# Four destinations side by side in one stationary operand for the last chunk of a count-matrix product

## The chip, the cores and the metric

The kernel runs on one core of a Trainium2 chip, as one program with one launch. The metric is device time in microseconds (us) for the whole program; lower is better. Outputs must agree with a JAX reference in float32.

## The reference, cut to what matters

Four graph-neural-network layers run one after the other on 3125 nodes with 128 features and 50000 edges, which are sorted by destination. Each is wrapped as `x = x + layer(relu(layernorm(x)))`. Layers 1 and 2 weight their edges by a softmax. Layer 0 (called gcn) and the two convolutions of layer 3 (sage1, sage2) need only a plain sum over the edges of each destination:

```python
h = features * rsqrt(max(deg_out, 1))[:, None]
h = h @ W
agg = segment_sum(h[edge_src], edge_dst)          # gcn
gcn_out = agg * rsqrt(max(deg_in, 1))[:, None] + b
...
agg = segment_sum(x[src], dst)                    # sage, twice
agg = agg / maximum(cnt, 1)[:, None]
h = agg @ Wl.T + x @ Wr.T + b
```

## The kernel before, in words

**Steps and chunks.** Destinations are taken in groups of `DG` = 4 (782 groups). The edges lie in 392 blocks of 128. A step is one pair of an edge block and a destination group, walked in order, so there are `STEPS` = 1172 steps. A chunk is 128 steps; there are `NC` = 10 chunks, and the last holds only 20 steps (24 with the padding of its last batch).

**The count matrix.** For every step and each of its four destinations `dl`, a column of the count matrix says how often each source node occurs. A chunk is stored as `adj[p, t*DG+dl, s]`: source node `t*128+p` (25 tiles `t`), destination `dl`, step `s`. TensorE builds it from one-hot vectors in 147 batches of 8 steps (L1389), ScalarE copies each batch into `adj` (L1015), which has two chunk buffers, and SyncE stores each finished chunk to `adj_hbm` (L700, 3200 KB each) for the layers that come later.

**The product.** A unit is one (chunk, `dl`) pair: 25 matmuls with `adj[:, ch, t*4+dl, :]` as the stationary operand (128 by 128) and node features, split in three bf16 parts, as the moving operand. In gcn (`spmm`, L1378) it streams 385 columns, the last of which gives counts. The ten chunks make 40 units, of which units 0 to 31 are placed between the build batches and units 32 to 39 run after the last batch. Before unit 39 the TensorE queue has the count products `degrees` (L1399) of chunks 0 to 8; that of chunk 9 follows after the last unit. VectorE takes each unit's result out of PSUM in `v_row` (a one-column copy, L1958, and a sum of the three parts, L1959). There are four PSUM banks for units, so unit n waits for `v_row(n-3)` to be counted in `v_done`.

**Selection.** `sel` (L1965, L1968) writes 0/1 matrices that say to which destination group each step belongs; `pick` (TensorE, L1449, 112 matmuls in float32) multiplies by them, which puts the sums in node order in `agg_t`. ScalarE copies its first four results out, VectorE the last four (L1975).

**The sage layers.** `load_adj` (SyncE, L819) streams the count matrix back from `adj_hbm` in 5 pieces a chunk, each 5 source tiles with their four destinations (640 KB), through a ring of `RING` = 9 buffers: 50 pieces a layer. A piece is loaded when the piece nine before it has been used (`spmm_done`). `stream` (L1468) runs 20 matmuls a piece, 1000 a layer, with four PSUM banks for even chunks and four for odd ones; VectorE reduces the four banks of a chunk after its last piece (L2386), and `pick` follows when all ten chunks are reduced.

**Between them** lie three edge passes (attn, gat1, gat2) of 98 groups of 512 edges, in which GpSimd gathers four blocks of rows a group (L984). Each engine has one queue, in program order; they meet in semaphores. The order of steps inside the layers is written out in tables of turns.

Of the kernel before, what the change touches and what calls it, by code (L numbers as in the profile page):

```python
# [6 lines left out]
F32 = mybir.dt.float32  # L7
BF16 = mybir.dt.bfloat16
# [5 lines left out]
P = 128  # L14
# [3 lines left out]
TURN = 4  # L18
# [26 lines left out]
PER = P // BATCH  # L45
NC = -(-STEPS // P)
SPAN = [(max(0, c * P - (CH - 2)), min(NGRP, (c + 1) * P)) for c in range(NC)]
SPAN_AT = [sum(b - a for a, b in SPAN[:c]) for c in range(NC + 1)]
HI = 5
NPR = NG // 2  # L50
# [6 lines left out]
HTURNS = -(-CH // WIDE)  # L57
DEG_LATE = NC - 1
RING = 9
assert NG % 2 == 0 and CH % QA == 0 and CQ <= P  # L60

# [94 lines left out]
def gnn_stack_kernel(nc, out, x, src, dst, edge_attr_64, **w):  # L156
    ctx = ExitStack()
    with ctx:
# [114 lines left out]
        def place(at, parts, *dims):  # L273
# [76 lines left out]
        late = carve(arena, {"v_rows": (P, (NC, DG, D), F32), "xs": (P, (NT, 3, D), BF16),  # L350
                             "sel": (P, (SPAN_AT[NC],), F32)}, late_v)
# [3 lines left out]
        sels = carve(arena, {"sel": (P, (SPAN_AT[NC],), F32), "sel_b": (P, (SPAN_AT[NC],), BF16)}, work_at)  # L355
        sel_early, sel_b = sels["sel"], sels["sel_b"]
# [65 lines left out]
        v_done = sem("v_done")  # L422
        sel_done = sem("sel_done")
        picked = sem("picked")
# [163 lines left out]
        def _(sp):  # L588
# [225 lines left out]
            def load_adj(i):  # L814

                def piece(n):
                    if i or n >= RING:
                        sp.wait_ge(spmm_done, NC * DG + i * NC * PIECES + n - RING + 1)
                    sp.dma_start(ring[:, (i * NC * PIECES + n) % RING, :],  # L819
                                 adj_hbm[n // PIECES, :, n % PIECES * HI * DG * P:(n % PIECES + 1) * HI * DG * P])\  # L820
                      .then_inc(adj_in[(i * NC * PIECES + n) % RING], 16)

                for n in range(NC * PIECES):
                    piece(n)

# [14 lines left out]
        def _(pool):  # L840
# [170 lines left out]
        def _(act):  # L1011
# [291 lines left out]
        def _(pe):  # L1303
# [126 lines left out]
            def pick(i, p):  # L1430

                pe.wait_ge(sel_done, i + 1)
                pe.wait_ge(v_done, [NC * DG, NC * DG + NC, NC * DG + 2 * NC][i])
                for half in range(2):
                    for dl in range(DG):
# [10 lines left out]
                        for ch in use:  # L1446
                            a0, a1 = max(SPAN[ch][0], g0), min(SPAN[ch][1], g1)
                            off = SPAN_AT[ch] - SPAN[ch][0]
                            i_ = mm(bank(half * 4 + dl)[:, a0 - g0:a1 - g0], v_of[p][:, ch, dl, :],  # L1449
                                    sel_of[p][:, off + a0:off + a1], start=ch == use[0], stop=ch == use[-1],  # L1450
                                    skip_group_check=True)
# [3 lines left out]
            def stream(i):  # L1455
                for n in range(NC * PIECES):
                    u = i * NC * PIECES + n
                    ch = n // PIECES
                    pe.wait_ge(adj_in[u % RING], 16 * (u // RING + 1))
                    if ch == 0:  # L1460
                        stage = "gat2" if i == 0 else "sage1"
                        pe.wait_ge(dve_o.sem, dve_o.at(stage, "r2", ((n + 1) * HI - 1) // TURN))
                    if n % PIECES == 0 and ch >= 2:
                        pe.wait_ge(v_done, NC * DG + i * NC + ch - 1)
                    for t in range(HI):
                        for dl in range(DG):
                            h = n % PIECES * HI + t
                            m = mm(bank(ch % 2 * 4 + dl)[:, 0:3 * D], ring[:, u % RING, (t * DG + dl) * P:(t * DG + dl + 1) * P],  # L1468
                                   xs1[:, h, :, :].rearrange("p s c -> p (s c)"), start=h == 0, stop=h == NT - 1)
                    m.then_inc(spmm_done, 1)  # L1470
# [259 lines left out]
        def _(dve):  # L1730
# [225 lines left out]
            def v_row(n):  # L1956
                dve.wait_ge(spmm_done, n + 1)
                v.tensor_copy(vdeg[:, n // DG, n % DG:n % DG + 1], bank(4 + n % 4)[:, 3 * D:3 * D + 1])  # L1958
                v.reduce_sum(v_early[:, n // DG, n % DG, :],  # L1959
                             bank(4 + n % 4)[:, 0:3 * D].rearrange("p (s c) -> p c s", s=3), axis=AX_X).then_inc(v_done, 1)  # L1960

            def sel(p):
                for ch in range(NC):
                    g0, g1 = SPAN[ch]
                    i = ts(sel_of[p][:, SPAN_AT[ch]:SPAN_AT[ch + 1]], grp_row[:, 0:g1 - g0], step_f[:, 1, ch:ch + 1], None,  # L1965
                           ALU.is_equal)
                    if p == "gcn":
# [31 lines left out]
            sel("gcn")  # L1999
            for k in range(done, NC * DG):  # L2000
                v_row(k)
# [378 lines left out]
            for i, p in enumerate(("sage1", "sage2")):  # L2380
                if i == 1:
                    dve.sem_inc(sel_done, 1)
                for ch in range(NC):
                    dve.wait_ge(spmm_done, NC * DG + (i * NC + ch + 1) * PIECES)
                    for dl in range(DG):
                        k = v.reduce_sum(v_late[:, ch, dl, :],  # L2386
# [44 lines left out]
```

## Time and profile before

| what | value |
|---|---|
| median of 3 runs | 3070.86 us |
| the three runs | 3072.97, 3061.61, 3070.86 us |
| the profiled execution, its own time | 3065.77 us |
| span of its trace | 3064.1 us |
| mean granted TensorE clock in it | 0.784 of full speed |
| TensorE busy | 2446.2 us (80%) |
| GpSimd busy | 1359.0 us (44%) |
| VectorE busy | 1385.8 us (45%) |

The span is from the first to the last instruction. Times inside it are counted from its start. PE is TensorE's matmul queue, PEld its weight loads, DVE is VectorE, ACT ScalarE, POOL GpSimd, SPq SyncE's queue of transfers. A line such as L1468 names the source line. An idle time stands in brackets, with what ended it. In the chain of waits each row is a piece of the path that ended last: its start, its length, and what ran.

### The profile page before, as it was taken

The numbers are of one execution on the slowest core, as the hardware profiler recorded it, in microseconds if no ns is written. First come the engines' busy times: TensorE is split into PE (matmuls) and PEld (weight loads), VectorE is DVE, ScalarE is ACT, GpSimd is POOL, SyncE is SP. The second block draws the span as 40 slices with busy tenths as digits, with TensorE's granted clock in tenths as the row PEclk, the third lists the DMA queues.
The fourth block names the chain that finished last, engine by engine and source line by source line (L and its number), as shares of the span: only waits on it lengthen the run. The fifth ranks groups of instructions, "written<-read, shape, count | busy, mean of one in ns | idle before, by whom it ended". The sixth has DMA issues, their size and how long they took to land.

```text
span 3064.1 us, 36766 instructions
## 1 busy us (share of the span) xinstructions
PE 2446.2 (80%) x12590; PEld 1810.7 (59%) x12590; DVE 1385.8 (45%) x3000; ACT 929.0 (30%) x1990; POOL 1359.0 (44%) x1416
## 2 busy tenths in 40 slices
PE   5699999848888897667788886666777775699998
PEld 5466666627777775455555554346777775366566
DVE  7655655356676766434445444232222223411313
ACT  4322222133333332543444443322222222201101
POOL 3000000077777773447777772437777773300000
PEclk7577778878898887767999998785555555799999
DMA  9877754039999995106777775205555553664460
GB/s 188 230 258 274 240 179 188 1 98 273 266 261 263 261 256 147 30 20 187 242 242 237 243 246 166 76 19 126 133 133 131 135 134 74 200 201 128 146 203 25
DMA packets 519442, 525.15 MB, mean 171 GB/s; under 512 B 154208, under 2 KB 463843, under 8 KB 517947
## 3 DMA queue, kind: packets, MB, share of 16 engines
q1 hardware_dynamic: 311425, 274.71, 30.1%
q0 software_dynamic: 50528, 115.22, 15.2%
q10 hardware_dynamic: 157306, 132.88, 13.8%
q8 instruction: 103, 1.69, 0.2%
q14 instruction: 80, 0.66, 0.1%
HBM read 306.05 MB, written 229.79 MB: 175 GB/s over the span
## 4 chain that ended last, share of the span: by engine, by line
PE 35%; POOL 32%; issue 13%; DVE 10%; DMA 5%; ACT 4%; another core or an unknown queue 1%; SPq 0%; POOLq 0%; PEldq 0%; DVEq 0%; ACTq 0%
POOL arena L984 30%; PE ps L1468 10%; PE ps L1378 7%; PE ps L1389 6%; DMA arena<-t_gat,src_i 3%; PE ps L1449 2%; DMA arena<-t_attn,src_i 2%; PE ps L1541 1%; PE ps L1665 1%; DVE arena L2160 1%; DVE arena L1840 1%; ACT arena L1015 1%; PE ps L1574 1%; PE ps L1704 1%; ACT arena L1258 1%
## 5 line engine op out<-in xcount | busy, mean ns | idle before, releaser
L1015 ACT ACTIVATE arena<-ps 128x544 f32<-128x544 f32 (+8 forms) x589 | 481.2, 826 | 1636.2 <-PE ps L1541 643.1
L984 POOL DMA_INDIRECT arena<-t_gat,src_i x784 | 740.6, 945 | 239.0 <-issue 233.5
L1541 PE MATMUL ps<-arena 128*128 128x136 f32 (+2 forms) x2352 | 649.7, 436 | 111.2 <-ACT arena L1015 57.5
L1541 PEld LDWEIGHTS ps<-arena 128*128 128x128 f32 x2352 | 447.2, 253 | 242.3 <-DVE arena L2160 89.1
L984 POOL DMA_INDIRECT arena<-t_attn,src_i x392 | 383.4, 978 | 119.5 <-issue 116.4
L1468 PE MATMUL ps<-arena 128*128 128x384 bf16 x2000 | 333.0, 331 | 33.9 <-DVE rec L2302 32.6
L1517 PEld LDWEIGHTS ps<-arena 128*128 128x128 f32 x1568 | 286.6, 267 | 32.2 <-ACT arena L1015 4.7
L1468 PEld LDWEIGHTS ps<-arena 128*128 128x128 bf16 x2000 | 197.9, 99 | 168.8 <-issue 43.0
L2108 DVE TENSOR_TENSOR z_b<-arena,ps 128x12 f32<-128x12 f32 (+1 forms) x196 | 31.5, 161 | 561.7 <-DMA arena<-t_gat,src_i 505.5
L1517 PE MATMUL ps<-arena 128*128 128x3 f32 (+1 forms) x1568 | 266.1, 292 | 4.2 <-ACT arena L1015 4.2
L947 POOL TENSOR_TENSOR arena<-arena,r_L_gnn_gamma 128x512 f32<-128x512 f32 (+1 forms) x7 | 8.0, 1150 | 556.9 <-ACT arena L1197 556.8
L1389 PE MATMUL ps<-arena 128*128 128x100 bf16 x1176 | 225.0, 364 | 27.7 <-DVE arena L1944 27.6
L1378 PE MATMUL ps<-arena 128*128 128x385 bf16 x1000 | 233.8, 407 | 0.0
L2160 DVE TENSOR_TENSOR arena<-arena,ps 128x1536 f32<-128x1536 f32 (+1 forms) x196 | 229.9, 1215 | 3.2 <-ACT arena L1134 2.5
L1389 PEld LDWEIGHTS ps<-arena 128*128 128x128 bf16 x1176 | 169.1, 146 | 78.3 <-DVE arena L1944 31.9
L1525 PE MATMUL ps<-ident,logit 128*64 128x128 f32 (+2 forms) x147 | 46.9, 319 | 172.9 <-DVE logit L2121 108.1
L1378 PEld LDWEIGHTS ps<-arena 128*128 128x128 bf16 x1000 | 119.6, 120 | 108.2 <-issue 69.2
L1015 ACT ACTIVATE arena<-same_b 128x512 f32<-128x512 bf16 x294 | 168.0, 620 | 25.4 <-DMA same_b<-same_hbm 25.3
L2098 DVE TENSOR_TENSOR arena<-arena,ps 128x1024 f32<-128x1024 f32 x98 | 119.1, 1215 | 122.3 <-DMA arena<-t_attn,src_i 93.3
L2386 DVE TENSOR_REDUCE arena<-ps 128x128 f32<-128x384 f32 x80 | 39.0, 549 | 274.1 <-PE ps L1468 274.1
L1525 PEld LDWEIGHTS ps<-ident,logit 128*64 128x64 f32 (+2 forms) x147 | 18.4, 125 | 183.1 <-DVE logit L2121 113.3
L1501 PE MATMUL ps<-w_e,arena 64*128 64x128 f32 x784 | 123.3, 302 | 0.7 <-DVE arena L2098 0.7
(315 smaller groups left out, 2930.3 us busy)
## 6 DMA issues: line engine op xcount, KB each, us to landing
ends_gat<-arena ACTq DMA_DIRECT2D x98, 774.0 KB, 4.3
arena<-adj_hbm SPq DMA_DIRECT2D x100, 640.0 KB, 3.9
same_b<-same_hbm SPq DMA_DIRECT2D x294, 128.0 KB
adj_hbm<-arena SPq DMA_DIRECT2D x10, 3200.0 KB, 11.4
ends_attn<-arena ACTq DMA_DIRECT2D x98, 272.0 KB, 4.7
ends_gat<-arena ACTq DMA_DIRECT2D x98, 258.0 KB, 3.7
arena<-edst SPq DMA_DIRECT2D x98, 256.0 KB, 4.1
starts_q<-zrow SPq DMA_DIRECT2D x28, 896.0 KB, 6.1
```

What stands on the lines that cost most here:

```text
L984: g.indirect_dma_start(out=row_b[:, n % RB, k, 0:row_tab[p].shape[1]], out_offset=None, in_=row_tab[p], in_offset=bass.IndirectOffsetOnAxi ...
L1015: return a.activation(o, i, ACT.Copy)
L1378: i = mm(bank(4 + n % 4)[:, 0:3 * D + 1], adj[:, ch % 2, t * DG + dl, :], xs0[:, t, 0:3 * D + 1], start=t == 0, stop=t == NT - 1)
L1389: i = mm(ps[:, at:at + KEYS], hot_e[:, b % 3, :, e], hot_k[:, b % 3, :, e], start=True, stop=True)
L1449: i_ = mm(bank(half * 4 + dl)[:, a0 - g0:a1 - g0], v_of[p][:, ch, dl, :], sel_of[p][:, off + a0:off + a1], start=ch == use[0], stop=ch == ...
L1468: m = mm(bank(ch % 2 * 4 + dl)[:, 0:3 * D], ring[:, u % RING, (t * DG + dl) * P:(t * DG + dl + 1) * P], xs1[:, h, :, :].rearrange("p s c - ...
L1501: i = mm(bank((1, 6)[g % 2])[:, k * D:(k + 1) * D], at_t[:, g % 2, k * P:(k + 1) * P], w_e[:, :], start=True, stop=True)
L1517: i = mm(ps[:, at:at + n_er], same_f[:, g % RB, k, :], er_c[:, g * GC + k, 0:n_er], start=True, stop=True)
L1525: nc.tensor.transpose(bank(2)[0:kh, 0:P], logit[:, i % 2, 0:kh], ident[:, :])\
L1541: i = mm(o, same_f[:, g % RB, k, :], msg[:, g % 4, k * W:(k + 1) * W], start=True, stop=True)
L2098: tt(kv, kv, bc(bank((1, 6)[g % 2]).rearrange("p (k s c) -> p k s c", k=GC, s=1), [P, GC, 2, D]), ALU.add).then_inc(kve_done.sem, 1)
L2160: tt(m[:, :, 0:heads * nc_].rearrange("p k (h c) -> p k h c", h=heads), rows_v, e, ALU.mult).then_inc(msg_done.sem, 1)
```

## The change

Only the last chunk is treated otherwise. Its 20 steps (24 with padding) fit in 32 columns, so its four destinations lie side by side in one 128-column stationary operand: column `dl*32+s`. It is one unit of 25 matmuls in place of four, its results come out with destination `dl` in partitions `dl*32` to `dl*32+31`, and `pick` reads this one result four times, each time with another selection matrix which is zero outside those partitions. gcn has 37 units, and each sage layer streams 47 pieces, of which the last two hold 13 and 12 tiles of the last chunk.

```diff
+LAST = P // DG
+UNITS = (NC - 1) * DG + 1
+ENDW = SPAN[NC - 1][1] - SPAN[NC - 1][0]
+SEL_W = SPAN_AT[NC] + (DG - 1) * ENDW
-DEG_LATE = NC - 1
+DEG_LATE = NC - 2
 RING = 9
+PIECE = [(c, t, t + HI) for c in range(NC - 1) for t in range(0, NT, HI)] + [(NC - 1, 0, 13), (NC - 1, 13, NT)]
+NPIECE = len(PIECE)
...
+        adj_end = adj[:, (NC - 1) % 2, :, :].rearrange("p k s -> p (k s)")[:, 0:KEYS * LAST]
...
             def store_adj(ch):
                 sp.wait_ge(adj_done, min(NB, (ch + 1) * PER))
-                sp.dma_start(adj_hbm[ch], adj[:, ch % 2, :, :].rearrange("p k s -> p (k s)")).then_inc(adj_out[ch % 2], 16)
+                if ch < NC - 1:
+                    o, i = adj_hbm[ch], adj[:, ch % 2, :, :].rearrange("p k s -> p (k s)")
+                else:
+                    o, i = adj_hbm[ch, :, 0:KEYS * LAST], adj_end
+                sp.dma_start(o, i).then_inc(adj_out[ch % 2], 16)
...
+                for n, (ch, t0, t1) in enumerate(PIECE):
+                    u, step = i * NPIECE + n, (DG * P if ch < NC - 1 else P)
+                    if u >= RING:
+                        sp.wait_ge(spmm_done, UNITS + u - RING + 1)
+                    sp.dma_start(ring[:, u % RING, 0:(t1 - t0) * step], adj_hbm[ch, :, t0 * step:t1 * step])\
+                      .then_inc(adj_in[u % RING], 16)
...
-            g.iota(step_i[:, 0, :], pattern=[[P, NC]], base=0, channel_multiplier=1)
+            g.iota(step_i[:, 0, 0:NC - 1], pattern=[[P, NC - 1]], base=0, channel_multiplier=1)
+            g.iota(step_i[:, 0, NC - 1:NC], pattern=[[0, 1]], base=(NC - 1) * P, channel_multiplier=1)
...
-                copy(adj[:, ch % 2, :, at:at + BATCH].rearrange("p k (s e) -> p k s e", s=2),
+                if ch < NC - 1:
+                    o = adj[:, ch % 2, :, at:at + BATCH]
+                else:
+                    o = adj_end.rearrange("p (k s) -> p k s", s=LAST)[:, :, at:at + BATCH]
+                copy(o.rearrange("p k (s e) -> p k s e", s=2),
...
-                    i = mm(bank(4 + n % 4)[:, 0:3 * D + 1], adj[:, ch % 2, t * DG + dl, :],
-                           xs0[:, t, 0:3 * D + 1], start=t == 0, stop=t == NT - 1)
+                    lhs = adj[:, ch % 2, t * DG + dl, :] if ch < NC - 1 else adj_end[:, t * P:(t + 1) * P]
+                    i = mm(bank(4 + n % 4)[:, 0:3 * D + 1], lhs, xs0[:, t, 0:3 * D + 1], start=t == 0, stop=t == NT - 1)
...
-            for n in range((NB // PER - 1) * DG + NB % PER // 4, NC * DG):
-                if n == NC * DG - 1:
+            for n in range((NB // PER - 1) * DG + NB % PER // 4, UNITS):
+                if n == UNITS - 1:
                     pe.wait_ge(sel_done, 1)
                     pe.wait_ge(adj_done, NB)
                     pe.wait_ge(v_done, DEG_LATE * DG)
                     for ch in range(DEG_LATE):
                         degrees(ch)
                 spmm(n // DG, n % DG)
-            pe.wait_ge(v_done, NC * DG)
-            degrees(NC - 1).then_inc(s_in, 1)
+            pe.wait_ge(v_done, UNITS)
+            for ch in range(DEG_LATE, NC):
+                i = degrees(ch)
+            i.then_inc(s_in, 1)
...
+                            if ch == NC - 1:
+                                off += dl * ENDW
+                            i_ = mm(bank(half * 4 + dl)[:, a0 - g0:a1 - g0], v_of[p][:, ch, dl if ch < NC - 1 else 0, :],
...
+                    for t in range(t0, t1):
+                        for dl in range(DG if ch < NC - 1 else 1):
+                            at = ((t - t0) * DG + dl if ch < NC - 1 else t - t0) * P
+                            m = mm(bank(ch % 2 * 4 + dl)[:, 0:3 * D], ring[:, u % RING, at:at + P],
+                                   xs1[:, t, :, :].rearrange("p s c -> p (s c)"), start=t == 0, stop=t == NT - 1)
...
-            v.tensor_copy(step_f[:, 0, :], step_i[:, 0, :])
+            v.tensor_copy(step_f[:, 0, 0:NC - 1], step_i[:, 0, 0:NC - 1])
+            for d in range(DG):
+                ts(step_f[d * LAST:(d + 1) * LAST, 0, NC - 1:NC], step_i[d * LAST:(d + 1) * LAST, 0, NC - 1:NC],
+                   float(-d * LAST), None, ALU.add)
+            v.memset(vdeg[:, NC - 1, :], 0.0)
...
-                v.tensor_copy(vdeg[:, n // DG, n % DG:n % DG + 1], bank(4 + n % 4)[:, 3 * D:3 * D + 1])
+                if n < UNITS - 1:
+                    v.tensor_copy(vdeg[:, n // DG, n % DG:n % DG + 1], bank(4 + n % 4)[:, 3 * D:3 * D + 1])
+                else:
+                    for d in range(DG):
+                        rows_d = slice(d * LAST, (d + 1) * LAST)
+                        v.tensor_copy(vdeg[rows_d, NC - 1, d:d + 1], bank(4 + n % 4)[rows_d, 3 * D:3 * D + 1])
...
             def sel(p):
+                v.memset(sel_of[p][:, SPAN_AT[NC - 1]:SEL_W], 0.0).then_inc(sel_zero, 1)
                 for ch in range(NC):
...
+                    else:
+                        dve.wait_ge(sel_zero, 1 if p == "gcn" else 2)
+                        for d in range(DG):
+                            rows_d, at = slice(d * LAST, (d + 1) * LAST), SPAN_AT[ch] + d * ENDW
+                            i = ts(sel_of[p][rows_d, at:at + ENDW], grp_row[rows_d, 0:ENDW], step_f[rows_d, 1, ch:ch + 1],
+                                   None, ALU.is_equal)
...
-                    dve.wait_ge(spmm_done, NC * DG + (i * NC + ch + 1) * PIECES)
-                    for dl in range(DG):
+                    dve.wait_ge(spmm_done, UNITS + i * NPIECE + LANDED[ch])
+                    for dl in range(DG if ch < NC - 1 else 1):
                         k = v.reduce_sum(v_late[:, ch, dl, :],
```

## Rows read from the trace of the kernel before

**Rows 1.** The profile's page: shares of the chain that ended last, by engine.

```profile
PE 35%; POOL 32%; issue 13%; DVE 10%; DMA 5%; ACT 4%; another core or an unknown queue 1%; SPq 0%; POOLq 0%; PEldq 0%; DVEq 0%; ACTq 0%
```

**Rows 2.** The chain of waits, end of gcn's product.

```profile
523.51 30.43 PE ps L1378 x175
553.94 1.48 PE ps L1399 x13
555.42 4.25 PE ps L1378 x25
...
559.69 0.16 DVE vdeg L1958
559.85 0.47 DVE arena L1959
```

**Rows 3.** The timeline there: start, length, engine, line, idle time before in brackets.

```profile
523.54 0.84 ACT L1015 ACTIVATE arena<-ps 128x800 bf16<-128x800 f32 x1 [0.62 <-PE ps L1389]
...
529.23 0.23 DVE L1965 TENSOR_SCALAR arena<-grp_row,step_f 128x20 f32<-128x20 f32 x1
...
529.51 0.15 DVE L1958 CAST vdeg<-ps 128x1 bf16<-128x1 f32 x1
529.58 0.54 DVE L1959 TENSOR_REDUCE arena<-ps 128x128 f32<-128x384 f32 x1
533.34 0.16 DVE L1958 CAST vdeg<-ps 128x1 bf16<-128x1 f32 x1 [3.22 <-PE ps L1378]
...
553.98 0.16 DVE L1958 CAST vdeg<-ps 128x1 bf16<-128x1 f32 x1 [3.50 <-PE ps L1378]
```

**Rows 4.** Chain of waits over the two sage layers.

```profile
2652.17 149.67 PE ps L1468 x920
2801.87 1.96 DVE arena L2386 x4
2803.96 23.15 PE ps L1449 x112
...
2849.25 165.13 PE ps L1468 x1000
3014.40 1.96 DVE arena L2386 x4
```

**Rows 5.** VectorE's timeline, the reductions of chunk 8 in sage2.

```profile
2998.15 1.95 DVE L2386 TENSOR_REDUCE arena<-ps 128x128 f32<-128x384 f32 x4 [14.30 <-PE ps L1468]
```

**Rows 6.** Line L2386 by itself: minimum, median, maximum in ns.

```profile
L2386 DVE TENSOR_REDUCE arena<-ps x80: 545/548/558, 2655.6 to 3015.8; 128x128 f32<-128x384 f32 x80
```

**Rows 7.** Stretches: length; PE, PEld, DVE, ACT, POOL busy; clock; DMA share; GB/s.

```profile
533.40:554.00 20.60, 20.60 (x127) 12.02 (x126) 3.09 (x11) 0.00 (x0) 0.00 (x0) 1.00 0.00 0
...
560.30:596.00 35.70, 34.70 (x170) 28.38 (x171) 12.30 (x41) 3.69 (x5) 0.00 (x0) 0.86 0.00 1
...
700.00:1200.00 500.00, 429.83 (x2812) 369.83 (x2811) 356.83 (x539) 179.06 (x435) 371.05 (x379) 0.88 0.92 256
...
2652.00:2802.00 150.00, 149.66 (x920) 89.95 (x920) 17.70 (x38) 0.00 (x0) 0.00 (x0) 1.00 0.65 201
```

**Rows 8.** VectorE's timeline at the start of the program.

```profile
11.46 0.69 DVE L1745 TENSOR_TENSOR arena<-arena 98x512 f32<-98x512 int32 x1 [5.59 <-DMA arena<-in_dst]
```

**Rows 9.** VectorE's timeline at the end of pass gat2.

```profile
2599.13 3.04 DVE L1965 TENSOR_SCALAR arena<-grp_row,step_f 128x128 f32<-128x128 f32 x10
2613.28 0.18 DVE L2302 TENSOR_SCALAR rec<-arena 128x4 f32<-128x4 f32 x1 [11.11 <-DMA arena<-ends_gat,end_i]
```

**Rows 10.** TensorE's timeline in pass attn.

```profile
798.60 2.18 PE L1541 MATMUL ps<-arena 128*128 128x136 f32 x8
...
805.43 0.42 PE L1525 MATMUL ps<-ident,logit 128*64 128x128 f32 x1
...
806.97 0.60 PE L1493 MATMUL ps<-ident,arena 128*64 128x128 f32 x4
...
810.90 0.60 PE L1493 MATMUL ps<-ident,arena 128*64 128x128 f32 x4
```

More of the change, by code:

```diff
@@ L46 @@
 NC = -(-STEPS // P)
+LAST = P // DG
+UNITS = (NC - 1) * DG + 1
+assert STEPS - (NC - 1) * P <= LAST and NB * BATCH - (NC - 1) * P <= LAST
 SPAN = [(max(0, c * P - (CH - 2)), min(NGRP, (c + 1) * P)) for c in range(NC)]
 SPAN_AT = [sum(b - a for a, b in SPAN[:c]) for c in range(NC + 1)]
+ENDW = SPAN[NC - 1][1] - SPAN[NC - 1][0]
+SEL_W = SPAN_AT[NC] + (DG - 1) * ENDW
 HI = 5
@@ L57 @@
 HTURNS = -(-CH // WIDE)
-DEG_LATE = NC - 1
+DEG_LATE = NC - 2
 RING = 9
+PIECE = [(c, t, t + HI) for c in range(NC - 1) for t in range(0, NT, HI)] + [(NC - 1, 0, 13), (NC - 1, 13, NT)]
+NPIECE = len(PIECE)
+LANDED = [max(i for i, q in enumerate(PIECE) if q[0] == c) + 1 for c in range(NC)]
 assert NG % 2 == 0 and CH % QA == 0 and CQ <= P
@@ L350, in gnn_stack_kernel @@
         late = carve(arena, {"v_rows": (P, (NC, DG, D), F32), "xs": (P, (NT, 3, D), BF16),
-                             "sel": (P, (SPAN_AT[NC],), F32)}, late_v)
+                             "sel": (P, (SEL_W,), F32)}, late_v)
         v_late, xs1, sel_late = (late[k] for k in ("v_rows", "xs", "sel"))
@@ L354, in gnn_stack_kernel @@
         v_early = carve(arena, {"v_rows": (P, (NC, DG, D), F32)}, vrow_at)["v_rows"]
-        sels = carve(arena, {"sel": (P, (SPAN_AT[NC],), F32), "sel_b": (P, (SPAN_AT[NC],), BF16)}, work_at)
+        sels = carve(arena, {"sel": (P, (SEL_W,), F32), "sel_b": (P, (SPAN_AT[NC],), BF16)}, work_at)
         sel_early, sel_b = sels["sel"], sels["sel_b"]
@@ L422, in gnn_stack_kernel @@
         v_done = sem("v_done")
-        sel_done = sem("sel_done")
+        sel_done, sel_zero = sem("sel_done"), sem("sel_zero")
         picked = sem("picked")
@@ L814, in load_adj @@
             def load_adj(i):
[L816 to L824, printed above, removed]
+                for n, (ch, t0, t1) in enumerate(PIECE):
[4 more added lines that the diff above has]
+                      .then_inc(adj_in[u % RING], 16)
             sp.wait_ge(s_steps, chains["x_gat2"].end)
@@ L1432, in pick @@
                 pe.wait_ge(sel_done, i + 1)
-                pe.wait_ge(v_done, [NC * DG, NC * DG + NC, NC * DG + 2 * NC][i])
+                pe.wait_ge(v_done, [UNITS, UNITS + NC, UNITS + 2 * NC][i])
                 for half in range(2):
@@ L1448, in pick @@
                             off = SPAN_AT[ch] - SPAN[ch][0]
-                            i_ = mm(bank(half * 4 + dl)[:, a0 - g0:a1 - g0], v_of[p][:, ch, dl, :],
+                            if ch == NC - 1:
+                                off += dl * ENDW
+                            i_ = mm(bank(half * 4 + dl)[:, a0 - g0:a1 - g0], v_of[p][:, ch, dl if ch < NC - 1 else 0, :],
                                     sel_of[p][:, off + a0:off + a1], start=ch == use[0], stop=ch == use[-1],
@@ L1455, in stream @@
             def stream(i):
-                for n in range(NC * PIECES):
-                    u = i * NC * PIECES + n
-                    ch = n // PIECES
+                for n, (ch, t0, t1) in enumerate(PIECE):
+                    u = i * NPIECE + n
                     pe.wait_ge(adj_in[u % RING], 16 * (u // RING + 1))
@@ L1461, in stream @@
                         stage = "gat2" if i == 0 else "sage1"
[L1462 to L1465, printed above, removed]
-                        for dl in range(DG):
-                            h = n % PIECES * HI + t
-                            m = mm(bank(ch % 2 * 4 + dl)[:, 0:3 * D], ring[:, u % RING, (t * DG + dl) * P:(t * DG + dl + 1) * P],
-                                   xs1[:, h, :, :].rearrange("p s c -> p (s c)"), start=h == 0, stop=h == NT - 1)
+                        pe.wait_ge(dve_o.sem, dve_o.at(stage, "r2", (t1 - 1) // TURN))
+                    if t0 == 0 and ch >= 2:
+                        pe.wait_ge(v_done, UNITS + i * NC + ch - 1)
+                    for t in range(t0, t1):
[3 more added lines that the diff above has]
+                                   xs1[:, t, :, :].rearrange("p s c -> p (s c)"), start=t == 0, stop=t == NT - 1)
                     m.then_inc(spmm_done, 1)
@@ L1962, in sel @@
             def sel(p):
+                v.memset(sel_of[p][:, SPAN_AT[NC - 1]:SEL_W], 0.0).then_inc(sel_zero, 1)
                 for ch in range(NC):
                     g0, g1 = SPAN[ch]
-                    i = ts(sel_of[p][:, SPAN_AT[ch]:SPAN_AT[ch + 1]], grp_row[:, 0:g1 - g0], step_f[:, 1, ch:ch + 1], None,
-                           ALU.is_equal)
+                    if ch < NC - 1:
+                        i = ts(sel_of[p][:, SPAN_AT[ch]:SPAN_AT[ch + 1]], grp_row[:, 0:g1 - g0], step_f[:, 1, ch:ch + 1],
+                               None, ALU.is_equal)
[4 more added lines that the diff above has]
+                            i = ts(sel_of[p][rows_d, at:at + ENDW], grp_row[rows_d, 0:ENDW], step_f[rows_d, 1, ch:ch + 1],
+                                   None, ALU.is_equal)
                     if p == "gcn":
@@ L1999, in _ @@
             sel("gcn")
-            for k in range(done, NC * DG):
+            for k in range(done, UNITS):
                 v_row(k)
@@ L2383, in _ @@
                 for ch in range(NC):
-                    dve.wait_ge(spmm_done, NC * DG + (i * NC + ch + 1) * PIECES)
-                    for dl in range(DG):
+                    dve.wait_ge(spmm_done, UNITS + i * NPIECE + LANDED[ch])
+                    for dl in range(DG if ch < NC - 1 else 1):
                         k = v.reduce_sum(v_late[:, ch, dl, :],
```

## The prediction

> **What bounds the kernel now.** I read the page first [rows 1]. The kernel is a row of stages with different limits: the chain that ended last is 35% TensorE, 32% GpSimd and 10% VectorE, so work taken off TensorE counts only where TensorE itself is that chain. The chain's own rows say where. In the tail of gcn's product TensorE runs 175 matmuls in 30.43 us, then the count products, then 25 more matmuls [rows 2]; in the sage layers it runs 920 and 1000 matmuls without a break [rows 4]. The change touches exactly these three places. The stretches say whether something else would take over at once: while sage1 streams, TensorE is busy 149.66 of 150 us at a granted clock of 1.00, and the DMA engines have a share of 0.65 at 201 GB/s [rows 7]. So the ring is ahead of its reader. VectorE is busy 17.7 us there, ScalarE not at all.
>
> **The change part by part: gcn.** Units 32 to 39 run after the build, 200 matmuls; 75 of them go. VectorE's copy L1958 starts when a unit is ready: for unit 33 at 533.34, for unit 38, five units on, at 553.98 [rows 3]. A unit costs 20.64 / 5 = 4.13 us, 165 ns a matmul. Three units are 12.4 us. They are the end of a row of units in which TensorE never idles, so the count products come earlier by all of it.
>
> What is given back there. First, `v_row` of the last unit makes four copies of 32 partitions instead of one of 128, and it lies on the chain: 0.16 us for the copy and 0.47 for what is left of the sum [rows 2]. In the timeline the sum L1959 starts 0.07 us after a copy that takes 0.15 [rows 3], so neighbours overlap. If all four copies overlap like this, three more cost some 0.24 us; if none overlaps with its neighbour, the four cost 4 x 0.16 = 0.64. No row shows a pair that starts at different partitions, so I take the middle, 0.4. The Trainium skill ("VectorE: DVE Perf Modes", section "Two Vector instructions with no wait between them") says that an instruction which starts in another group of 32 partitions than the one before is held until that one has finished. No row of before can confirm it; by it the upper end holds and the whole gain is 0.2 us smaller.
>
> Second, the count product of chunk 8 moves from before the last unit to behind it: one matmul of 1.48 / 13 = 0.11 us [rows 2], which costs nothing if it only changes place, or 0.11; I take 0.1. Together the count products come 12.4 - 0.4 - 0.1 = 11.9 us earlier.
>
> Edits in gcn that I cost at nothing, each with its cover:
> - `sel`: a memset and three more short comparisons, at most 4 x 0.23 = 0.9 us. It delays `v_row` of unit 32, now at 529.51 [rows 3]. Unit 36, now the last, waits for that; TensorE reaches it only after unit 35 (533.34 + 2 x 4.13 = 541.6) and 12 count products, at 543. The slack is over 10 us; without it the cost would be these 0.9 us.
> - The store of the last chunk is a quarter as long and starts at the same time. VectorE and ScalarE wait for the stores before they overwrite `adj`, after the count products. From 533.4 us on the DMA engines move nothing [rows 7], 14 us before the count products would now end.
> - ScalarE's three copies into the new layout write with another stride. The last ends at 524.4 [rows 3], 18 us before TensorE reads it. Even at twice their 0.84 us they are covered.
> - At the start of the program: one more iota on GpSimd, and a memset and four short operations on VectorE. VectorE then waits 5.59 us for the destinations [rows 8]. Uncovered this would be about 1 us.
>
> Does the 11.9 us survive? Behind the count products the chain goes through `pick`, linear products, normalisation and the first scatters, and none of these waits for a transfer that was started before: from 560.3 to 596 the DMA share is 0.00 [rows 7]. The passes are paced by GpSimd's gathers, which begin when gcn's tables are written. So everything shifts by it.
>
> **The sage layers.** The last chunk runs 25 matmuls instead of 100. The reductions of chunks 8 and 9 start at 2998.15 [rows 5] and 3014.40 [rows 4], so a chunk costs 16.25 us, 162.5 ns a matmul. Three quarters of it are 12.2 us a layer. The 25 now add to one PSUM bank in a row, where `stream` walked over four. gcn's units have done this all along, at 165 ns for 385 columns; by that figure the price is at most 25 x 2.5 ns = 0.06 us, and I take none.
>
> At the layer's end `pick` waits for four reductions, 1.96 us on the chain [rows 4]. Now it waits for one, of 0.55 us [rows 6]. Those of chunk 8 (1.95 us) run while TensorE works 25 x 0.1625 = 4.1 us on chunk 9, which covers them by 2.1 us. This saves 1.4 us a layer.
>
> Chunk 9 is read in pieces of 13 and 12 tiles, 416 and 384 KB instead of five times 640. Bytes and matmuls fall by the same factor, so a stream bound by its transfers would gain as much. Between the streams lie 2849.25 - 2801.84 = 47 us [rows 4], in which nine pieces for sage2 land, as before. `sel` for sage has a memset and three more comparisons (0.9 us at most); VectorE idles 11.11 us behind it [rows 9]. `pick` keeps its 112 matmuls.
>
> Sum: 11.9 + 2 x 12.2 + 2 x 1.4 = 39.1 us. The profiled execution took 3065.77 us (its span and 1.7 around it) and would take 3026.7. The median of the runs is 5.1 us above it, which gives 3031.8. The four times of before have a mean of 3067.8. I take this as the level: 3028.7, so 3029.
>
> **The rivals.**
> *Only the sage layers gain.* gcn's shift is lost in a pass behind it. For it speaks that GpSimd is 32% of the chain. Against it: the first gather waits for gcn's results, and nothing in a pass runs by a clock of its own. Time 3067.8 - 27.2 = 3040.6; 7 in 100.
>
> *The clock in pass attn falls (the slower side).* The granted clock from 700 to 1200 us is 0.88 [rows 7], a mix of the levels 1.2 and 2.4 GHz. At the lower a group of edges takes TensorE 805.43 - 798.60 = 6.8 us, at the upper 810.90 - 806.97 = 3.9 [rows 10]. The gathers pace the pass with 500 / (379 / 4) = 5.3 us a group [rows 7]. With a share s of the pass at the lower level TensorE needs 3.9 + 2.9 s: s is now 0.24, which makes 4.6. It becomes the bound beyond s = 0.48, a clock of 0.76. To end 0.5% above before it must lose 39 + 15 = 54 us over 98 groups, 0.55 a group: s = 0.67, a clock of 0.66. Wholly at the lower level it loses 1.5 x 98 = 147 us, for 3176. Against it: the pass does the same work in the same order and only starts earlier. 3 in 100. The Trainium skill ("TensorE: Matmul & The Clock Gate", section "Part 1: The HAM clock gate") holds that sustained activity releases the lower clock; the trace agrees so far, with 1.00 in the dense stream of sage1 against 0.88 in this pass. By that rule unchanged work keeps its clock.
>
> *The stream does not get shorter.* Chunk 9's larger pieces come late, or the ring sets the pace at the layer's end, and TensorE waits out what it saves. Only gcn's part is left: 3067.8 - 11.9 = 3055.9. The DMA share of 0.65 [rows 7] and the unbroken 1000 matmuls [rows 4] speak against it. 2 in 100.
>
> **How the numbers follow.** The forecast gets 88 in 100. With all small costs at their lower end the gain is 39.4 us; at their upper end, and nothing covered (0.9 and 1 us in gcn, 0.9 in sage), 36.0. So most of the width is the kernel's own: 3061.6 to 3073.0 before gives 3022 to 3037. Another mix of the two clock levels in the stretches around gcn's end (0.86, [rows 7]) is worth some 5 us to either side; that makes 3017 to 3042, which takes in the rival that only sage gains and leaves out under 2 in 10. Below I allow 1 us more, 3016. Faster by over 0.5% (15 us, about what a measurement of this kernel can tell from no change): 0.95. Within it: 0.02, the third rival. Slower: 0.03, the second.
>
> **What would show it.** Right: L1378 falls from 1000 matmuls to 925, L1468 from 2000 to 1850; behind the build 125 matmuls instead of 200; the count products end 11.9 us earlier; each unbroken stretch of L1468 is 12.2 us shorter; one L2386 stands before `pick`. Wrong: idle time in front of L1468 in chunk 9; a group of pass attn over 5.3 us at a lower clock; another length from the count products to the first gather.

## The result and the profile after

The changed kernel takes 3030.13 us (median of 4 runs, 3028.73 to 3030.65), the kernel before 3070.96 (4 runs, 3061.61 to 3072.97). The ratio is 0.9873, with a 95% interval of 0.986 to 0.9885: 39.0 us less on 3070.96 (35.3 to 43.0). The forecast was 3029, its range 3016 to 3042.

The chain of waits of the changed kernel around the end of gcn's product, which answers to [rows 2] (L1394 is now `spmm`, L1414 `degrees`, L1985 and L1986 `v_row`, L1468 `pick`):

```profile
522.45 18.04 PE ps L1394 x100
540.49 1.41 PE ps L1414 x12
541.90 4.25 PE ps L1394 x25
...
546.18 0.15 DVE vdeg L1985
...
546.34 0.15 DVE vdeg L1985
...
546.51 0.16 DVE vdeg L1985
...
546.68 0.17 DVE vdeg L1985
...
546.86 0.57 DVE arena L1986
...
547.48 0.24 PE ps L1414 x2
547.72 11.61 PE ps L1468 x56
```

Behind the build there are 125 matmuls instead of 200. The four copies stand one after the other, 0.17 us from start to start, and the sum starts 0.68 us after the first of them. From the last build batch to the first matmul of `pick` it is 547.72 - 522.45 = 25.27 us, where it was 560.54 - 523.51 = 37.03. The end of that stretch before, behind the last row of [rows 2]:

```profile
560.37 0.17 PE ps L1399
560.54 11.61 PE ps L1449 x56
```

The same chain over the sage layers, which answers to [rows 4] (L1486 is `stream`, L2421 the reduction):

```profile
2644.10 137.49 PE ps L1486 x845
2781.61 0.57 DVE arena L2421
2782.32 23.15 PE ps L1468 x112
...
2827.60 152.99 PE ps L1486 x925
2980.62 0.57 DVE arena L2421
2981.32 23.15 PE ps L1468 x112
```

The unbroken stretches are 149.67 - 137.49 = 12.2 and 165.13 - 152.99 = 12.1 us shorter, and one reduction stands before `pick` where there were four. VectorE's timeline at the end of sage2, which answers to [rows 5]:

```profile
2976.56 1.95 DVE L2421 TENSOR_REDUCE arena<-ps 128x128 f32<-128x384 f32 x4 [14.30 <-PE ps L1486]
2980.62 0.56 DVE L2421 TENSOR_REDUCE arena<-ps 128x128 f32<-128x384 f32 x1 [2.11 <-PE ps L1486]
```

Chunk 9 takes 4.06 us, 25 matmuls of 162.4 ns. Chunk 8's reductions are done 2.1 us before it ends.

GpSimd's gathers mark the borders of the stages behind gcn. The views of their lines give the first and the last start of each. Before (L984 are the gathers in the passes, L993 those that follow a pass), and then in the changed kernel (L995 and L1004):

```profile
L984 POOL DMA_INDIRECT arena<-t_gat,src_i x784: 940/944/1114, 1377.6 to 2558.4; - x196
L984 POOL DMA_INDIRECT arena<-t_attn,src_i x392: 942/946/1462, 683.7 to 1185.3; - x196
```

```profile
L993 POOL DMA_INDIRECT arena<-ends_gat,end_i x50: 939/944/2180, 1937.8 to 2635.5; - x50
L993 POOL DMA_INDIRECT arena<-ends_attn,end_i x25: 938/944/1221, 1230.5 to 1261.3; - x25
```

```profile
L995 POOL DMA_INDIRECT arena<-t_gat,src_i x784: 940/944/1112, 1366.3 to 2550.1; - x196
L995 POOL DMA_INDIRECT arena<-t_attn,src_i x392: 942/946/1462, 672.2 to 1174.0; - x196
```

```profile
L1004 POOL DMA_INDIRECT arena<-ends_gat,end_i x50: 939/946/2153, 1929.8 to 2627.4; - x50
L1004 POOL DMA_INDIRECT arena<-ends_attn,end_i x25: 940/944/1143, 1219.4 to 1250.0; - x25
```

With the same marks in both traces (us from the span's start, and the change of each stage's length; the first matmul of `stream` is the first start in the view of its line):

| the stage ends with | before | changed | change of its length |
|---|---|---|---|
| the last build batch | 523.5 | 522.5 | -1.1 |
| the first matmul of gcn's `pick` | 560.5 | 547.7 | -11.8 |
| the first gather of pass attn | 683.7 | 672.2 | +1.4 |
| the first gather behind pass attn | 1230.5 | 1219.4 | +0.3 |
| the first gather of pass gat1 | 1377.6 | 1366.3 | -0.2 |
| the first gather behind pass gat1 | 1937.8 | 1929.8 | +3.3 |
| the first matmul of `stream` | 2630.2 | 2622.1 | -0.1 |
| the first matmul of sage2's `pick` | 3016.5 | 2981.3 | -27.1 |
| the span | 3064.1 | 3028.9 | 0.0 |

The two stages that were edited give 38.9 us. The trace as a whole gives 35.2, because stages that were not edited have other lengths in the two traces, pass gat1 most of all, and then the stage from gcn's `pick` to the first gather of pass attn. So two questions were left for experiments: do the parts add up as the sum says, and are the 3.3 us of pass gat1 and the 1.4 us in front of pass attn costs of the change or differences between executions?

### The profile page after: what moved, and what is told of

Its sections match the earlier page's. It is cut to its first block, busy times and chain, and to the rows that moved or that the text cites. A ratio compares the mean times of both kernels' runs of the same rounds, so it can differ in the third digit from the quotient of the medians.

```text
span 3028.9 us, 36312 instructions
## 1 busy us (share of the span) xinstructions
PE 2409.3 (80%) x12365; PEld 1785.7 (59%) x12365; DVE 1382.3 (46%) x3004; ACT 927.9 (31%) x1990; POOL 1359.2 (45%) x1417
## 4 chain that ended last, share of the span: by engine, by line
PE 36%; POOL 31%; issue 12%; DVE 11%; DMA 6%; ACT 4%; another core or an unknown queue 1%; SPq 0%; POOLq 0%; PEldq 0%; DVEq 0%; ACTq 0%
POOL arena L995 29%; PE ps L1486 10%; PE ps L1394 7%; PE ps L1404 6%; DMA arena<-t_gat,src_i 3%; PE ps L1468 2%; DMA arena<-t_attn,src_i 2%; PE ps L1559 2%; DVE arena L2195 2%; PE ps L1683 1%; DVE arena L1862 1%; ACT arena L1026 1%; PE ps L1660 1%; PE ps L1592 1%; PE ps L1722 1%
## 5 line engine op out<-in xcount | busy, mean ns | idle before, releaser
L995 POOL DMA_INDIRECT arena<-t_gat,src_i x784 | 740.6, 945 | 238.9 <-issue 232.5
L995 POOL DMA_INDIRECT arena<-t_attn,src_i x392 | 383.6, 979 | 119.5 <-issue 114.0
L1486 PE MATMUL ps<-arena 128*128 128x384 bf16 x1850 | 307.1, 330 | 35.4 <-DVE rec L2337 34.1
L2143 DVE TENSOR_TENSOR z_b<-arena,ps 128x12 f32<-128x12 f32 (+1 forms) x196 | 31.3, 160 | 548.8 <-DMA arena<-t_gat,src_i 495.6
L1486 PEld LDWEIGHTS ps<-arena 128*128 128x128 bf16 x1850 | 182.6, 99 | 159.7 <-issue 43.0
L1394 PE MATMUL ps<-arena 128*128 128x385 bf16 x925 | 220.3, 412 | 0.0
L1404 PEld LDWEIGHTS ps<-arena 128*128 128x128 bf16 x1176 | 169.2, 146 | 78.5 <-DVE arena L1966 32.2
L1394 PEld LDWEIGHTS ps<-arena 128*128 128x128 bf16 x925 | 111.9, 121 | 102.6 <-issue 68.2
L2421 DVE TENSOR_REDUCE arena<-ps 128x128 f32<-128x384 f32 x74 | 36.2, 551 | 249.7 <-PE ps L1486 249.7
L1519 PE MATMUL ps<-w_e,arena 64*128 64x128 f32 x784 | 123.2, 301 | 1.1 <-DVE arena L2133 0.9
## 6 DMA issues: line engine op xcount, KB each, us to landing
adj_hbm<-arena SPq DMA_DIRECT2D x9, 3200.0 KB, 12.1
```

Source lines behind the costliest of these rows:

```text
L995: g.indirect_dma_start(out=row_b[:, n % RB, k, 0:row_tab[p].shape[1]], out_offset=None, in_=row_tab[p], in_offset=bass.IndirectOffsetOnAxi ...
L1394: i = mm(bank(4 + n % 4)[:, 0:3 * D + 1], lhs, xs0[:, t, 0:3 * D + 1], start=t == 0, stop=t == NT - 1)
L1404: i = mm(ps[:, at:at + KEYS], hot_e[:, b % 3, :, e], hot_k[:, b % 3, :, e], start=True, stop=True)
L1519: i = mm(bank((1, 6)[g % 2])[:, k * D:(k + 1) * D], at_t[:, g % 2, k * P:(k + 1) * P], w_e[:, :], start=True, stop=True)
```

## The experiments

Lines are numbered as in the changed kernel unless said. The median of the kernel before, timed beside each, is given with it.

**The change in gcn alone.** The sage layers go back to four products for the last chunk. Their weights still come from the packed store, so its bytes are a quarter.

```diff
-PIECE = [(c, t, t + HI) for c in range(NC - 1) for t in range(0, NT, HI)] + [(NC - 1, 0, 13), (NC - 1, 13, NT)]
+PIECE = [(c, t, t + HI) for c in range(NC) for t in range(0, NT, HI)]
...
-                        for dl in range(DG if ch < NC - 1 else 1):
-                            at = ((t - t0) * DG + dl if ch < NC - 1 else t - t0) * P
+                        for dl in range(DG):
+                            at = ((t - t0) * DG + dl) * (P if ch < NC - 1 else LAST)
```

> The change in gcn alone. In both sage layers the last chunk is again four products of 25 matmuls (its weights are read from the packed store, in five pieces), with four reductions. Theory (TensorE is the chain in all three places and the parts add): the gain is gcn's 11.9 us against before, and the kernel is 27.2 us slower than the changed one, so about 3030 + 27 = 3057; 100 matmuls in the last chunk take 16.25 us. Rival (gcn's shift is lost in a pass behind it): level with before, so the 40 us between the medians would all be sage's. Rival (the stream was held by its transfers): with a quarter of the bytes in the last chunk, its four products would take less than 16.25 us.

Measured: 3062.95 us against 3073.15, ratio 0.9969 (0.9957 to 0.9981), so a gain of 9.5 us (5.8 to 13.2). Its chain of waits at gcn's end and in sage2:

```profile
522.85 18.04 PE ps L1394 x100
...
542.30 4.25 PE ps L1394 x25
...
548.11 11.61 PE ps L1468 x56
...
2848.57 165.13 PE ps L1486 x1000
3013.73 1.96 DVE arena L2421 x4
```

gcn's part is there, 548.11 - 522.85 = 25.26 us from the last build batch to `pick`, and the whole run keeps it: level with before is outside the interval. sage2 takes the 165.13 us of before although a quarter of the bytes of its last chunk are read, so the transfers did not set its pace. The time is 5.9 us above the expected 3057; the kernel before stood 2.2 us higher in this series than in the first, and the interval holds the 11.9 us of the theory.

**The change in the sage layers alone.** gcn has 40 units again.

```diff
-UNITS = (NC - 1) * DG + 1
+UNITS = NC * DG
...
-                    lhs = adj[:, ch % 2, t * DG + dl, :] if ch < NC - 1 else adj_end[:, t * P:(t + 1) * P]
+                    lhs = adj[:, ch % 2, t * DG + dl, :] if ch < NC - 1 else adj_flat[:, (t * DG + dl) * LAST:(t * DG + dl) * LAST + P]
```

> The change in the two sage layers alone. gcn has 40 units again, four of them for the last chunk (whose weights are read from the packed layout). Theory: the gain against before is 27.2 us, and the kernel is 11.9 us slower than the changed one, about 3042. Rival (gcn's shift is lost behind it): level with the changed kernel, 3030.

Measured: 3043.23 us against 3073.15, ratio 0.9898 (0.9883 to 0.9913), so 31.3 us (26.7 to 36.0), which holds the 27.2 of the theory. Its chain (L1395, L1469, L1487 and L2420 in this kernel's numbering):

```profile
525.68 30.43 PE ps L1395 x175
...
562.72 11.61 PE ps L1469 x56
...
2844.52 152.98 PE ps L1487 x925
2997.53 0.57 DVE arena L2420
```

gcn's end takes 562.72 - 525.68 = 37.04 us as before, and sage2 is that of the changed kernel. The rival, level with the changed kernel, is excluded. The two halves together gain 9.5 + 31.3 = 40.8 us, against 39.0 for the whole change (35.3 to 43.0): they add, within the width of these intervals.

**The matmuls back, the rest kept.** The last chunk's 25 matmuls run four times in each of the three places.

```diff
-                for t in range(NT):
+                for t in [t for _ in range(DG if ch == NC - 1 else 1) for t in range(NT)]:
...
+                            for extra in range(3 if ch == NC - 1 else 0):
+                                mm(bank(ch % 2 * 4 + 1 + extra)[:, 0:3 * D], ring[:, u % RING, at:at + P],
+                                   xs1[:, t, :, :].rearrange("p s c -> p (s c)"), start=t == 0, stop=t == NT - 1)
```

> The changed kernel, but the 25 matmuls of the last chunk run four times in each of the three places (in gcn into the same bank, where the last pass counts; in sage into three banks that nobody reads). Everything else of the change stays: one v_row, one reduction, 47 pieces. Theory (the matmuls are nearly all of the gain): 3 x 12.3 = 37 us slower than the changed kernel, about 3067; the one reduction before pick stays, so it keeps 2.8 us of the gain less 0.5 for the four copies. Rival (fewer reductions, fewer pieces or a shorter store carry a good part): clearly less than 37 us slower.

Measured: 3067.32 us against 3073.15, ratio 0.9987 (0.9977 to 0.9997), a gain of 4.0 us (0.9 to 7.1) where the theory left 2.3. Its chain (`stream`'s own matmuls are L1489 here; the stretch shown ends before the last chunk):

```profile
542.25 16.63 PE ps L1394 x100
...
560.44 11.61 PE ps L1468 x56
...
2845.56 147.93 PE ps L1489 x900
...
3009.77 0.57 DVE arena L2424
```

The unit is 16.63 - 4.25 = 12.4 us longer, and the last chunk of sage2 takes 3009.77 - 2845.56 - 147.93 = 16.3 us instead of 4.06. The matmuls are nearly all of the gain. Fewer reductions, pieces and bytes together are worth the few us that stay.

**Five pieces instead of two for the last chunk.**

```diff
-PIECE = [(c, t, t + HI) for c in range(NC - 1) for t in range(0, NT, HI)] + [(NC - 1, 0, 13), (NC - 1, 13, NT)]
+PIECE = [(c, t, t + HI) for c in range(NC - 1) for t in range(0, NT, HI)] + [(NC - 1, t, t + HI) for t in range(0, NT, HI)]
```

> The changed kernel with the last chunk read in five pieces of five tiles instead of two of 13 and 12. Theory (the ring is far ahead of TensorE): no change, 3030 within the noise, and the last 25 matmuls take 4.06 us as in the changed kernel. Rival (the number of pieces matters): slower by up to the landing time of one transfer, 3.9 us a layer, with idle time in front of the matmuls of chunk 9.

Measured: 3030.69 us against 3073.15, ratio 0.9868 (0.9853 to 0.9883). VectorE's timeline, and from the chain of waits sage2's stream:

```profile
2974.37 1.95 DVE L2421 TENSOR_REDUCE arena<-ps 128x128 f32<-128x384 f32 x4 [14.30 <-PE ps L1486]
2978.43 0.56 DVE L2421 TENSOR_REDUCE arena<-ps 128x128 f32<-128x384 f32 x1 [2.11 <-PE ps L1486]
```

```profile
2828.08 150.32 PE ps L1486 x925
```

Chunk 9 takes 4.06 us again, with no idle time of TensorE in front of it. Five pieces or two makes no difference that can be told; the ring is ahead. The stream as a whole took 150.32 us here and 152.99 in the changed kernel. The 2.7 us lie at its start: in its first 10 us the granted clock was 1.00 here and 0.74 there, and 1.00 in both behind that.

**The kernel before, a second trace.** Nothing is edited.

> The kernel before, unchanged, for a second trace. The four runs of before spread over 11.4 us, the profiled one lay 5 us under their median. Theory (the spread comes from the mix of clock levels in stages that TensorE bounds in part): the stages from the last build batch to the first gather and the three passes differ from the first trace by some us each, while the sage streams repeat to 0.1 us. Rival: the spread lies in the transfers.

Measured: one time, 3065.85 us, with 3071.1 as the median of seven others. Its chain, and its gathers in and behind the passes gat1 and gat2:

```profile
522.14 28.89 PE ps L1378 x175
...
2849.57 164.87 PE ps L1468 x1000
```

```profile
L984 POOL DMA_INDIRECT arena<-t_gat,src_i x784: 940/944/1116, 1373.5 to 2559.1; - x196
```

```profile
L993 POOL DMA_INDIRECT arena<-ends_gat,end_i x50: 940/946/1834, 1936.0 to 2634.0; - x50
```

The same 175 matmuls took 28.89 us here and 30.43 in [rows 2]. So the stretch from the last build batch to `pick` itself varies by 1.5 us between executions, and that it came out 11.8 us shorter is read from two traces in which TensorE lost the same time there: the changed kernel's 100 matmuls took 18.04 us, and 16.51 in three of the other traces (the kernel with the matmuls back, and of those below the one with four times the transposes and the one with the masked product). Pass gat1 took 1936.0 - 1373.5 = 562.5 us against 560.2 in the first trace. Over the ten traces of this study it took 560.2 to 564.2 us, with the first trace of before at the lower end and the changed kernel's 563.5 inside. Among the seven with the change in gcn it was 560.3 to 564.2, among the three without it 560.2 to 562.5; the means are 0.9 us apart. So most of the 3.3 us is a difference between executions; a cost of a microsecond is not excluded. Sage2's stream of 1000 matmuls repeated to 0.3 us, not the expected 0.1, in three traces, but the one of 925 did not: 150.32 to 152.99 us in six. The rival, that the spread lies in the transfers, was not tested. That the clock makes the spread in that pass was not shown: its granted clock was 0.89 both in the first trace of before and in the changed kernel's, so this stays open.

The 1.4 us in front of pass attn are another matter. From gcn's `pick` to the first gather it took 121.7 to 123.2 us in the four kernels' traces in which gcn still runs all its matmuls (before twice, the sage layers alone, the matmuls back), and 123.8 to 124.6 us in the six in which 75 of them are gone. It holds the linear products behind gcn, 50 matmuls of 512 columns (L1642 before, L1660 changed): on average 774 to 792 ns each in the four, and 835 to 837 in five of the six (837 in the changed kernel), that is, with more of their time at the lower clock level. In the sixth, the kernel with four times the transposes, they took 790 ns and the stage 123.8 us. So some 1 to 2 us of gcn's gain were lost there in every trace. What makes the clock meet them at the lower level was not tested.

**More TensorE work in pass attn.** The slower rival rested on how much TensorE has to spare there. The transposes of the edge attributes run twice (and, in a second kernel, four times) for each group.

```diff
-                    for k in range(GC):
+                    for k in [k for _ in range(2) for k in range(GC)]:
                         i = nc.tensor.transpose(bank(0)[0:ED, k * P:(k + 1) * P], at_b[:, g % UNROLL, k, :], ident[:, :])
```

> The changed kernel with the four transposes of the edge attributes run twice for each group of pass attn: 0.60 us more TensorE work a group at the upper clock level, 1.06 at the lower. Theory of the prediction (gathers pace the pass, TensorE has 5.3 - 4.6 = 0.7 us to spare): the pass does not get longer, or by less than 10 us. Rival (TensorE is close to the bound): longer by up to 98 x 0.7 = 69 us.

> The same with the four transposes run four times: 1.8 us more a group at the upper level, 3.2 at the lower. Theory: TensorE needs 4.6 + 2.1 = 6.7 us a group at the present mix of levels, which is 1.4 over the gathers' 5.3, so the pass is 98 x 1.4 = 137 us longer. If the busier engine is granted the upper level throughout: 3.9 + 1.8 = 5.7, 0.4 over, 40 us.

Measured against 3071.1: 3032.49 us for twice (ratio 0.987, 0.9853 to 0.9886), and 3039.62 us for four times (0.9902, 0.9885 to 0.9919). The first costs nothing that can be told; its pass took 545.4 us, at a granted clock of 0.90. The second costs 0.9902 - 0.9873 = 0.0029 of 3071, 8.9 us, where 137 or 40 were expected; the two intervals just touch. Its four times reach from 3031.0 to 3044.11 us, and the trace is of the fastest. The pass in the changed kernel, and then with four times the transposes (length; PE, PEld, DVE, ACT, POOL busy; clock; DMA share; GB/s):

```profile
672.20:1219.40 547.20, 450.80 (x2906) 382.65 (x2906) 369.09 (x561) 187.09 (x447) 383.66 (x393) 0.85 0.87 243
```

```profile
671.10:1222.10 551.00, 523.86 (x4082) 474.98 (x4082) 369.56 (x561) 196.62 (x447) 380.58 (x392) 0.95 0.85 242
```

And TensorE's timeline in the second:

```profile
799.11 1.09 PE L1559 MATMUL ps<-arena 128*128 128x136 f32 x8
...
804.26 1.19 PE L1559 MATMUL ps<-arena 128*128 128x136 f32 x8
805.29 1.91 PE L1511 MATMUL ps<-ident,arena 128*64 128x128 f32 x16
...
809.32 1.09 PE L1559 MATMUL ps<-arena 128*128 128x136 f32 x8
```

Three things were wrong in the expectation. The granted clock did not stay at its mix: it went from 0.85 to 0.95 over the pass as TensorE's busy time rose from 450.80 to 523.86 us. And a set of four transposes does not cost its duration: four sets take 1.91 us where one takes 0.60 [rows 10], so three more cost 1.3 and not 1.8, since the tail of one overlaps the next. And the gathers' pace is not 5.3 us a group. That figure divides a window up to 1200 us, but the last gather of the pass starts at 1185.3: 391 gaps in 1185.3 - 683.7 us are 5.13 us a group. With four times the transposes two groups take 809.32 - 799.11 us, 5.1 each, and from 750 to 1150 us TensorE never idles, at a granted clock of 1.00. So it just keeps the gathers' pace there. The gathers themselves are done as soon (671.1 to 1169.9 us, against 672.2 to 1174.0), and the pass is 551.0 - 547.2 = 3.8 us longer because it ends 52.2 us behind its last gather where it was 45.4. Where the slower executions lose the rest of the 8.9 us no trace shows.

**One masked product for the four copies, and the last chunk's unit earlier.** The mask stands in `vdeg` from the start; the units behind the build run in the order 32, 33, the last chunk's, 34, 35.

```diff
-                    for d in range(DG):
-                        rows_d = slice(d * LAST, (d + 1) * LAST)
-                        v.tensor_copy(vdeg[rows_d, NC - 1, d:d + 1], bank(4 + n % 4)[rows_d, 3 * D:3 * D + 1])
+                    tt(vdeg[:, NC - 1, :], bc(bank(4 + n % 4)[:, 3 * D:3 * D + 1], [P, DG]), vdeg[:, NC - 1, :], ALU.mult)
...
-                spmm(n // DG, n % DG)
+                spmm(*at_place(n))
```

> The changed kernel with two edits at the end of gcn's product: the four copies of the last unit's counts are one product with a 0/1 mask, and the last chunk's unit runs third of the five behind the build, so that it is not the one that the count products wait for. Theory: the four copies, 0.67 us on the chain in the changed kernel, become an ordinary copy of 0.08 to 0.16, so the count products come about 0.5 us earlier, too little for the whole time to show. Rival: a later chunk's unit in the middle waits for the last build batch and costs more than it brings.

Measured: 3028.97 us against 3071.1, ratio 0.9867 (0.9851 to 0.9883), 1.2 us under the changed kernel's median and not to be told from it. The product with the mask in VectorE's timeline, and the chain (L1406 is `spmm`, L1426 `degrees`, L1480 `pick`):

```profile
537.00 0.16 DVE L1999 TENSOR_TENSOR vdeg<-ps,vdeg 128x4 bf16<-128x4 f32 x1 [3.50 <-PE ps L1406]
```

```profile
542.50 4.25 PE ps L1406 x25
...
546.77 0.16 DVE vdeg L1997
546.93 0.47 DVE arena L2000
...
547.45 0.24 PE ps L1426 x2
547.69 11.61 PE ps L1480 x56
```

From the end of the last unit to `pick` it is 547.69 - 546.75 = 0.94 us instead of 547.72 - 546.15 = 1.57: 0.6 us, about what was expected. The masked product takes 0.16 us, as one copy does, and it is no longer on the chain; as both edits were made at once, the 0.6 us is that of the two together. The rival did not show: between 523 and 549 us TensorE waits for nothing but that last sum, 0.7 us. By its trace it is better at this place; the whole time does not show it.

## Why the prediction was right, step by step

**What bounds the kernel.** Right. In all three places the chain got shorter by what was taken off TensorE (in gcn less what the four copies gave back), and with the matmuls put back only 4.0 us of the gain were left.

**Three units in gcn, less the four copies and a count product: 11.9 us.** Measured 11.8. Up to the end of the last unit the chain is (30.43 + 1.48 + 4.25) - (18.04 + 1.41 + 4.25) = 12.5 us shorter, and from there to `pick` it is 1.57 us instead of 560.54 - 559.67 = 0.87, so 0.7 longer. The term for the copies was sized 0.4 between 0.24 and 0.64, and it was 0.6: from the first copy to the end of the sum it is 547.43 - 546.18 = 1.25 us instead of 0.16 + 0.47 = 0.63. The copies do not overlap, and the sum does not overlap the last of them either, so the upper end was the one to take. The Trainium skill says ("VectorE: DVE Perf Modes", section "Two Vector instructions with no wait between them") that an instruction in another group of 32 partitions is held until its predecessor has finished; the four rows at 0.17 us spacing agree. The moved count product only changed place: 1.48 - 1.41 = 0.07 us less before the last unit, 0.24 - 0.17 = 0.07 more behind it.

**75 matmuls a sage layer: 12.2 us each.** Measured 12.2 and 12.1. 25 accumulations in a row into one PSUM bank run at 162.4 ns, as the walk over four did. **Reductions: 1.4 us each.** 1.96 became 0.57. Together the stages of the two layers are 27.1 us shorter, for 27.2. That these agree to 0.1 us is in part luck of the pair of traces: sage2's 925 matmuls took up to 2.7 us less in other executions.

**The edits at nothing.** `sel`, the smaller store, the copies' new layout and the pieces do not appear on the chain of the changed kernel; for the pieces and the bytes the experiments show it too. Unit n waits for `v_row` of unit n-4, the last user of its bank, so unit 36 waits for that of unit 32, as the prediction has it (the description of the kernel before says n-3, which is the count in `v_done`); it starts at 529.33 us in the changed kernel, over 12 us before unit 36.

**The shift survives.** Right in the main: a lead of 12.8 us at gcn's `pick` arrives as 11.3 at the first gather of pass gat1. "So everything shifts by it" was not exact. "Another length from the count products to the first gather" was one of the prediction's signs of being wrong, and it came: 124.5 us instead of 123.1, and over 123.7 in all six shortened kernels, in five of them with the same matmuls at a lower mix of the clock levels. The range had 5 us for such a mix; the sum had nothing. What is lost in pass gat1 is mostly its spread.

**The level.** The profiled executions differ by 3065.77 - 3030.65 = 35.1 us, the medians by 40.8, and the sum says 39.1. To take the gain off the mean of all times of before, and not off the profiled one alone (3026.7), brought the number within 1.1 us. Some of that is luck: the level of 3067.8 was 3.2 us under the median that before then had (3070.96), and the gain was 1.7 us under the difference of the medians. The two errors go against each other.

**The rivals.** *Only the sage layers gain*: excluded by the kernel with gcn's part alone. *The stream does not get shorter*: excluded by the chain, and by the stream that kept its 165.13 us on a quarter of the last chunk's bytes. *The clock in pass attn falls*: it did not, 0.85 over the pass in both. Its price was built on a reserve of 5.3 - 4.6 = 0.7 us a group at a fixed mix of the levels, and that step was wrong twice. The gathers' pace is 5.13 us, so the reserve was 0.5, and at the lower level throughout the pass would lose 6.8 - 5.1 = 1.7 us a group (an estimate), not 1.5. And the mix is not fixed: with more work in a group the granted clock rose from 0.85 to 0.95, and the pass grew by 3.8 us. That is the direction of the Trainium skill's rule in "TensorE: Matmul & The Clock Gate" ("Part 1: The HAM clock gate"), by which activity releases the lower clock. What would lower the clock in this pass, and what the pass would then cost, no run here shows.

## What to carry to other kernels

A padded tail block costs TensorE as much as a full one: here the last chunk, with 20 steps, took the same 16.25 us as chunk 8 with 128 (14.30 + 1.95 in [rows 5]). Look for the product whose stationary operand is mostly empty, put several side by side, each with partitions of its own in the result, and let the selection that follows separate them. Then ask of each place whether TensorE is the chain there, and compare stage by stage between fixed marks, since the spread of untouched stages can hide a tenth of such a gain.

## What the runs showed of the hardware that was not expected

- Four copies of 32 partitions by one column, each in another quarter of the partitions, took 0.68 us to the start of the next instruction. One copy of 128 partitions takes 0.16, and its successor starts 0.07 us after the copy's own start [rows 3]; a product with a mask over all partitions takes 0.16 too.
- In pass attn, 1.3 us more TensorE work on a group of 3.9 made the pass 3.8 us longer in the one traced execution, the fastest of four, with the granted clock up from 0.85 to 0.95; by the medians the whole time grew by 8.9 us.
- 25 matmuls in a row into one PSUM bank took 162.4 ns each, as a walk over four banks did (162.5).
- With 75 matmuls gone from gcn, the 50 matmuls of the linear products behind it took 835 to 837 ns on average in five traces of six, where they took 774 to 792 in the four with all matmuls. Why the clock meets them so is open.
- Pass gat1, with the same instructions, took 560.2 to 564.2 us in ten executions. A stream of 925 matmuls took 150.32 to 152.99 us in six; between the shortest and the changed kernel's the granted clock differs in its first 10 us, 1.00 against 0.74.
